# Attention values on TensorE: the order of the DMA-turned pair and of the pair that TensorE turned

## The reference

```python
qkv = (x @ qkv_w.T).reshape(Bb, Ss, 3, H, D)          # H = 16 heads, D = 64
q, k, v = ...                                         # rotary embedding on q and k
scores = jnp.einsum('bhqd,bhkd->bhqk', q, k) * SCALE
kb = -p * jnp.log1p(a * dist)                         # a bias by head and distance
attn = jax.nn.softmax(scores + kb[None], axis=-1)
out = jnp.einsum('bhqk,bhkd->bhqd', attn, v)
return out.reshape(Bb, Ss, H * D) @ out_w.T
```

## Time and profile before

| what | us |
|---|---|
| median of three runs | 1271.6 |
| the profiled execution's own time | 1268.28 |
| its span, first to last instruction | 1266.5 |
| TensorE busy with matmuls in it | 1096.5 (87%) |
| VectorE, ScalarE, GpSimd busy | 1016.0, 1002.6, 818.2 |
| chain that ended last: TensorE, DMA, GpSimd, ScalarE | 38%, 12%, 9%, 6% |

### The profile page before, as it was taken

One profiled execution on the slowest core, in us unless ns is written; L12 is line 12 of the kernel. 1 busy time (PEld: TensorE's weight loads), 2 busy tenths in 40 slices (PEclk: granted clock), 3 DMA queues, 4 the chain that ended last, 5 costly groups with the idle time before them and its releaser, 6 DMA issues.

```text
span 1266.5 us, 35475 instructions
## 1 busy us (share of the span) xinstructions
PE 1096.5 (87%) x14436; PEld 798.3 (63%) x14436; DVE 1016.0 (80%) x2061; ACT 1002.6 (79%) x1987; POOL 818.2 (65%) x481
## 2 busy tenths in 40 slices
PE   5740799999479999999999998999999999999874
PEld 5730688898146666666666765666666666666653
DVE  7873799997468788878878887887998788788872
ACT  2684688885169889889889897888998898899991
POOL 3035100000279888898889788888888888888741
PEclk9985799999899999999999999999999999999997
DMA  8715576762126556656755584676567557555573
GB/s 259 273 48 206 182 240 226 236 228 103 33 43 126 110 101 122 131 90 114 131 122 94 114 143 89 102 130 122 102 102 155 98 98 130 127 97 101 111 122 75
DMA packets 390289, 165.79 MB, mean 131 GB/s; under 512 B 340722, under 2 KB 380671, under 8 KB 390128
## 3 DMA queue, kind: packets, MB, share of 16 engines
q1 hardware_dynamic: 377856, 143.26, 53.2%
q0 software_dynamic: 4352, 12.41, 2.9%
q10 hardware_dynamic: 7920, 7.87, 2.0%
HBM read 58.79 MB, written 21.00 MB: 63 GB/s over the span
## 4 chain that ended last, share of the span: by engine, by line
PE 38%; DMA 12%; POOL 9%; ACT 6%; issue 5%; DVE 3%; SPq 1%; another core or an unknown queue 1%; POOLq 0%; ACTq 0%
PE ps_x L1303 9%; PE ps_s L1347 8%; PE ps_o L1378 7%; PE ps_t L1358 6%; PE ps_x L1322 5%; DMA pt_dma<-prob_parts 5%; DMA ot<-ctx_parts 4%; ACT prob L1114 3%; PE ps_x L1313 3%; POOL rot L989 2%; DMA res<-in_L_attn_x_dram 2%; POOL prob_parts L999 2%; POOL got L1016 1%; POOL ctx_parts L1007 1%; ACT pt_pe L1098 1%
## 5 line engine op out<-in xcount | busy, mean ns | idle before, releaser
L1224 DVE CUSTOM_DVE_ANT_0 prob<-ps_s,strips,score_scale 128x512 f32<-128x512 f32 x512 | 360.3, 746 | 10.1 <-PE ps_s L1347 9.4
L1114 ACT ACTIVATE prob<-prob,neg_max 128x512 f32<-128x512 f32 x512 | 364.1, 714 | 2.1
L999 POOL TENSOR_TENSOR prob_parts<-prob,prob_parts 128x1024 f16<-128x1024 f32 x128 | 273.3, 2135 | 84.5 <-ACT prob_parts L1104 84.3
L1230 DVE SCALAR_TENSOR_TENSOR pt_pe<-ps_t,pt_pe 128x1024 f16<-128x1024 f32 x128 | 156.0, 1219 | 54.3 <-ACT pt_pe L1098 54.3
L1347 PE MATMUL ps_s<-parts 32*128 32x512 f16 x3072 | 194.7, 383 | 0.2
L1303 PE MATMUL ps_x<-xcur,wqkv_hi 128*128 128x512 f16 x512 | 156.7, 388 | 36.8 <-ACT proj L1076 20.6
L989 POOL TENSOR_TENSOR rot<-prods 128x1024 f32<-128x1024 f32 x62 | 146.5, 2363 | 12.2 <-DVE parts L1267 11.7
L1358 PEld LDWEIGHTS ps_t<-ident,prob 128*128 128x128 f32 x1024 | 109.8, 141 | 64.0 <-issue 40.2
L1358 PE MATMUL ps_t<-ident,prob 128*128 128x128 f32 x1024 | 139.8, 279 | 8.2 <-DVE pt_pe L1230 8.2
L993 POOL TENSOR_TENSOR parts<-rot,parts 128x1024 f16<-128x1024 f32 x62 | 132.6, 2139 | 6.3 <-ACT parts L1093 6.3
L1104 ACT CAST prob_parts<-prob 128x1024 f16<-128x1024 f32 x128 | 133.7, 1044 | 2.0
(11 more groups left out here) (190 smaller groups left out, 2600.0 us busy)
## 6 DMA issues: line engine op xcount, KB each, us to landing
raw<-in_L_ffn_w_dram SPq DMA_DIRECT2D x32, 1024.0 KB, 5.1
xa<-in_L_attn_x_dram SPq DMA_DIRECT2D x8, 512.0 KB, 6.5
xt_dram<-xth SPq DMA_DIRECT2D x8, 512.0 KB, 5.1
slots_dram<-zeros SPq DMA_DIRECT2D x4, 1024.0 KB, 8.3
xa<-slots_dram SPq DMA_DIRECT2D x16, 256.0 KB, 5.3
expert_dram<-xa POOLq DMA_DIRECT2D x16, 256.0 KB, 6.8
xcur<-xt_dram SPq DMA_DIRECT2D x8, 512.0 KB, 4.3
res<-in_L_attn_x_dram ACTq DMA_DIRECT2D x8, 512.0 KB, 4.0
```

The costliest lines, as they stand in the source:

```text
L999: nc.gpsimd.tensor_tensor(prob_parts[:, n % 2, 1], prob[:, (2 * n + 1) % 3], prob_parts[:, n % 2, 0], ALU.subtract).then_inc(prob_lo, 1)
L1114: nc.scalar.activation(prob[:, s % 3, q, :], prob[:, s % 3, q, :], ACT.Exp, bias=neg_max[:, 2 * (s % 3) + q:2 * (s % 3) + q + 1], scale=-1 ...
L1224: nc.vector.tensor_tensor_reduce(prob[:, s % 3, q, :], ps_s[u][:], strips[:, HG * j + u, start:start + S], score_scale[:, 0:1], 3.0e38, AL ...
L1230: nc.vector.scalar_tensor_tensor(out=pt_pe[:, n % 2, 1].rearrange("p q k c -> p q (k c)"), in0=ps_t[:], scalar=P_SCALE, in1=pt_pe[:, n % 2 ...
```

## The change

In `quad`, in TensorE's list, the two calls change places:

```diff
                 fill_for(b, 2 * q)
                 if n >= 2:
+                    values(n - 2, 1)
+                if n >= 2:
                     values(n - 2, 0)
-                if n >= 2:
-                    values(n - 2, 1)
                 fill_for(b, 2 * q + 1)
```

## The result

The changed kernel takes 1283.99 us (median of four runs, 1281.2 to 1287.12) against 1271.73 us for the kernel before (median of four, 1269.08 to 1276.42): 12.3 us more, a ratio of 1.0093 with a 95% interval of 1.0055 to 1.0131. On the chip of the first four experiments it was run again: 1284.81 against 1269.66 us, 15.2 us more, ratio 1.0132 (1.0105 to 1.0159). So the change costs 12 to 15 us, about 1.1%; the two intervals reach from 7 to 20 us. The forecast was 1284 us and 13 us more.

What follows compares the result with a forecast made beforehand. TensorE, 94% busy in attention, was taken as the bound. Late landings cost between 9.1 us (13 chain steps) and 17.0 us (by groups of four); 13 was taken, and 1271.6 + 13 gave 1284 us, range 1276 to 1297.

Steps and rivals of the forecast that it cites:

- What bounds: In attention TensorE is 94% busy with almost no room; its pt_dma waits, 13.0 us in 15, lie on the chain.
- 0.70 us for each late landing: At the value matmuls, the first pair no longer hides 0.70 us of the DMA wait; each late landing costs up to that.
- Nothing comes back: First pair's data are ready early and pv_done counts both pairs, so the new order serves nobody sooner; no gain.
- The ends of the sum, 9.1 and 17.0, and the choice of 13: Chain's 13 steps at 0.70 give 9.1 us; largest piece per group of four gives 17.0; 13 taken between.
- The share of the late quads: Quads with n%4 = 1, behind a context turn in SyncE's queue, hold 14.4 of the 24.7 us of missing pieces.
- The count of 50 late landings: Of quads 0 to 125, 50 landings come late for the new place, adding up to 24.7 us.
- Groups of four share slack: TensorE's delay at an n%4 = 1 quad gives the next quad's DMA room; largest piece per group leaves 17.0 us.
- The reason for that slack: SyncE, issuing the DMAs, waits for GpSimd 107 times, 339.8 us, and for TensorE's values 70 times, 57.0 us.
- What would show it: pt_dma waits of 25 to 35 us in 35 to 50, median below 0.7; more than 13 chain steps through pt_dma.
- the fourth rival: Transposing DMAs land about 0.8 us sooner at all 13 chain steps, -1.3 us, 1270 us, not slower; chance 0.06.
- The clock: Two pt_dma waits grow to 2.46 and 2.94 us; half-clock stretches after one or two would add 1.7 to 3.4 us.
- the clock rival: Half-clock stretches follow four or five of TensorE's longer waits: 21.5 us more, 1293 us; chance 0.1.

Runs made afterwards that it cites:

- the first four experiments: Against the kernel before: whole change again +15.2 us; order changed only in n%4 = 1 quads +10.6; only in the others +5.9; half the pair moved +3.5.
- without the landings: Both pairs read pt_pe, no TensorE wait for pt_dma: 1259.4 us in the old order, 1257.44 in the new, against 1272.07 for the kernel before.
- the place 2.01 us earlier: DMA-turned pair put ahead of the fill before the values, wait 2.01 us earlier than in the kernel before: 1395.98 us, +123.9 us, ratio 1.1004.
- the cut DMA: Each quad's transposing DMA cut into high and low part: old order 1281.19 us against 1265.83 for the kernel before, new order 1301.02 us.
- the late quads alone: Order changed only for the values of quads with n%4 = 1, against the kernel before: 1280.28 us, +10.6 us, ratio 1.0096.

## Why the prediction was right, step by step

- **What bounds.** TensorE's order sets the time, and most of a wait for `pt_dma` is on the path: shown, by the 12.7 us that leave with the landings, and by the profiled pair, where 16.6 us more waiting made attention 16.9 us longer.
- **0.70 us for each late landing.** Shown in the timeline, 1.41 us of matmuls behind the landing in place of 0.71 us.
- **Nothing comes back.** Shown within the noise: without the landings the two orders differ by -2.0 us, inside the intervals.
- **The ends of the sum, 9.1 and 17.0, and the choice of 13.** The runs gave 12.3 and 15.2 us, the profiled pair 16.9 us in attention. The lower end held, and the upper one lies inside the second interval. The choice of 13 between them was a judgement, not a sum, and that it came within 1 us of the first measurement is in part luck: that one is known to about 5 us, and the second gave 15.2. What `proj` and `ot` swallowed is 2.9 us in the profiled pair, close to the 4 us between 17.0 and 13, but `turned_lo`, which the prediction had shrinking, grew by 1.5 us. The share of the late quads, 14.4 of 24.7 us, was measured as 10.6 of 16.5, and as 13.2 of the 16.6 us of waits. The count of 50 late landings was too high for the kernel as it then ran: in its trace the first value matmul starts within 0.12 us of the landing in 34 of the quads 0 to 125.
- **Groups of four share slack.** Supported, by the waits of the quads behind the late ones, 9.6 us where the late quads don't wait first and 3.9 us where they do. With the place 2.01 us earlier it still held, and the late quad's own part was undersized.
- **The reason for that slack**, that SyncE waits for GpSimd and rarely for TensorE, was right, and more so than the row says: in 118 of the 128 quads the issue follows GpSimd's end by less than 0.15 us, so the 70 waits for TensorE's values ended before the one for GpSimd. For the late quads the reason was incomplete. In 9 of the 31 late quads of the kernel before, the issue came 0.23 to 1.52 us behind GpSimd's end, because SyncE was still issuing the context's turn ahead of it. SyncE's own 1.3 to 3.5 us for that issue is part of why these quads are late, and the cut DMA failed on it.
- **What would show it.** 29.6 us against "some 25 to 35" came out; 31 waits against "35 to 50" did not (the view leaves out gaps under 0.15 us), nor did a median below 0.7 us: it is 0.79. So fewer quads wait than was counted, and each for longer. The chain holds more steps, as named, and the landings have not become shorter, with a median of 4.7 us against 4.6, which speaks against the fourth rival.
- **The clock.** Half-clock stretches (1.2 GHz in place of 2.4) did follow two of the longer waits, of 2.54 and 2.48 us. TensorE's timeline at both, and the granted clock right behind them:

```profile
1007.38 0.20 PE L1378 MATMUL ps_o<-val_hi,pt_dma 128*128 128x64 f16 x1 [2.54 <-DMA pt_dma<-prob_parts]
...
1218.67 0.20 PE L1378 MATMUL ps_o<-val_hi,pt_dma 128*128 128x64 f16 x1 [2.48 <-DMA pt_dma<-prob_parts]
```

```profile
1007.70:1011.00 3.30, 3.30 (x49) 2.93 (x46) 1.00 (x3) 0.65 (x3) 1.97 (x1) 0.50 0.78 150
1219.30:1222.60 3.30, 3.30 (x53) 2.12 (x53) 1.58 (x3) 1.91 (x6) 0.00 (x0) 0.50 0.83 158
```

That is the "one or two" of the prediction, 1.7 us each, but it came out partly by luck: of the two waits that the prediction made longer, that of 1.76 us became 1.27 and only that of 2.24 us grew, to the 2.48 here; the one of 2.54 us stands at a quad that did not wait before. But between the first scores and the drain of the last quads such stretches were six in the kernel before and five in this one, because three and not six came with the waits for `proj`. After one of those, as long as 2.68 us, the clock stayed at full level:

```profile
431.73 0.39 PE L1303 MATMUL ps_x<-xcur,wqkv_hi 128*128 128x512 f16 x1 [2.68 <-ACT proj L1076]
```

```profile
431.80:436.00 4.20, 3.97 (x40) 1.94 (x41) 3.37 (x5) 4.13 (x11) 4.20 (x3) 1.00 0.93 176
```

So in this pair the clock added nothing on balance; TensorE's busy time says the same, 842.71 against 841.69 us. Other executions had more of them: seven in that of the change run again, and those named above with the late quads alone, the wait still earlier and the cut DMA. So the clock rival was of the right kind, and small here. The Trainium skill's rule in TensorE: Matmul & The Clock Gate, Part 1, that an idle TensorE falls back to the throttled level, agrees with the two rows at 0.50. The one at 1.00, behind a longer wait, shows that the length of the wait alone did not decide it here.

## What to carry to other kernels

Where an engine's list has two independent pieces and one waits for something slow, the ready piece goes first: its own length is cover, and if the engine is the one that sets the time, moving it behind the wait costs up to that length at each late arrival, less where one wait gives the next arrivals slack. Count the late arrivals at the new place, not the waits of today; a place that moves forward makes waits that no row of the old profile shows. Before moving a wait back to gain cover, or cutting a transfer to make it land sooner, look at what stands behind it in every other engine's list and in the issuing queue.

## What was not expected of the hardware

SyncE spends time on each transposing DMA that no busy share shows: 1.3 to 3.7 us (median 2.0) for one of the probabilities in the kernel before, and 1.24 us (median) for a half. The landing of a half takes 3.4 us against 4.6, so halving the data took 1.2 us off the landing and added about half a microsecond to the two issues together (2.5 against 2.0 us). In a queue that holds several in a row this turned a faster transfer into a later landing.
